# The mean made once, inner values on 128 partitions, and a diagonal in two parts, in the LayerNorm of a four-layer kernel

## The chip, the cores and the metric

The kernel runs on one core of a Trainium2 chip. The metric is device time in microseconds of that core, median of the timed runs. A core has TensorE (PE, with its weight load PEld), VectorE (DVE), ScalarE (ACT), GpSimd (POOL) and SyncE (SP), each with its own instruction queue worked off in order.

## The reference

Input x is 8 sequences of 256 tokens of 256 values. Four layers each add to it: L0 (two routed ReLU experts and three shared ones, mixed by a gate), L1 (eight SiLU-gated experts and a shared one), L2 and L3. The change lies in L2, and in one place where L0 ends:

```python
h = relu(x @ w1[lang] + b1[lang])          # 256 -> 64
y = x + h @ w2[lang] + b2[lang]            # 64 -> 256
mean = jnp.mean(y, axis=-1, keepdims=True)
var = jnp.mean(jnp.square(y - mean), axis=-1, keepdims=True)
x = x + (y - mean) * rsqrt(var + 1e-5) * gamma[lang] + beta[lang]
x = x + x @ W3[subject].T + b3[subject]    # L3
```

## The kernel before

Activations are held transposed, features on 128 partitions in two tiles (`dt` 0 and 1), tokens along the free dimension. Most products are made in fp32r from a high and a low part of each operand: `xh` and `xl` are rounded x and the rest, and `product` (L435 to L437) issues high by high, high by low, low by high. ScalarE makes high parts, VectorE or GpSimd the low parts (`lo_part`, L1440).

The last phase runs L1's shared expert over five jobs (`LAST_JOBS`): three of 512 tokens and two of 256, eight steps each, T = 0 to 39. In step T TensorE issues `last_up(T)` (12 products), then `last_down(T-2)` (6 products), then the hooks of T. VectorE in step T makes the gated tile and its low part (`last_tile`), and in the first step of a job, inside `last_tile`, `last_take` of the job before, which waits for all of its down products and adds them to x. Then come its hooks. Steps 40 and later hold only the rest. As `last_down` lags two steps, TensorE issues the last down products of a job in the second step of the next one.

L2 and L3 are hung in as hooks per unit (unit 0 to 4 = job 0 to 4). The table `WHEN` gives for each unit the step T of each stage, in the order of `STAGES`, and every engine takes its own stages of step T, ordered by unit, then by stage: x2 (high ScalarE, low VectorE), xs (row sum of x in two parts, units 1 and 2: GpSimd, ScalarE, GpSimd), up (TensorE, 64 rows out), hid (ScalarE ReLU twice: plain into `ru`, rounded into `u`; VectorE the low part), down (TensorE), res (VectorE adds x and bias), square (VectorE, GpSimd), scale (ScalarE), var (TensorE), eps (VectorE, then GpSimd takes the power -0.5), diag (ScalarE: identity times the inverse deviation, 128x128 for every 128 tokens), rstd (TensorE spreads it over the partitions), norm and add (VectorE), x3 (high) and x3l (low), l3a and l3b (TensorE), outa and outb (VectorE). Units 0 to 2 use the PSUM pair `sums[0]`, unit 3 `up_ps[:, 2:4]`.

The weights W2 are centred, so that only the mean of x has to be taken off. In the down stage (`l2_down_stage`) `mean_part` adds -1/256 times the column sums of x to both output tiles, and the three products with the 64-row weights follow. b2 is centred in `center_b2` (VectorE, step 10). Unit 4, `END`, is spread over the steps from 42 on in a form of its own.

L0's mix of the last 512 tokens is made by VectorE inside L1's first pairs, k = 0 to 3 (`pair_tiles`): `gate_probs` and `mix`.

## Time and profile before

| | |
|---|---|
| median of 3 runs | 1599.67 us (1598.49 to 1599.91) |
| the profiled execution, device time | 1598.26 us |
| its span, first to last instruction | 1596.5 us |
| TensorE busy | 1583.3 us, 99% |
| VectorE / ScalarE / GpSimd busy | 71% / 58% / 41% |
| mean granted TensorE clock, DMA | 1.000, mean 54 GB/s |

Busy times add up overlapping matmuls, so 99% does not say that TensorE is at its peak. The chain of waits says what the end hangs on, and the list of waits says where an engine stood still and which instruction ended it. In a timeline a line gives start, duration, engine, source line and, in brackets, the idle time ahead of it and who ended it.

### The profile page before, as it was taken

The numbers are of one execution on the slowest core, as the hardware profiler recorded it, in microseconds if no ns is written. First come the engines' busy times: TensorE is split into PE (matmuls) and PEld (weight loads), VectorE is DVE, ScalarE is ACT, GpSimd is POOL, SyncE is SP. The second block draws the span as 40 slices with busy tenths as digits, with TensorE's granted clock in tenths as the row PEclk, the third lists the DMA queues.
The fourth block names the chain that finished last, engine by engine and source line by source line (L and its number), as shares of the span: only waits on it lengthen the run. The fifth ranks groups of instructions, "written<-read, shape, count | busy, mean of one in ns | idle before, by whom it ended". The sixth has DMA issues, their size and how long they took to land.

```text
span 1596.5 us, 22398 instructions
## 1 busy us (share of the span) xinstructions
PE 1583.3 (99%) x7944; PEld 1345.9 (84%) x7944; DVE 1138.5 (71%) x1676; ACT 930.0 (58%) x1680; POOL 662.1 (41%) x576
## 2 busy tenths in 40 slices
PE   9999999999999999999999999999999999999999
PEld 7888888999987888888888888888888888888888
DVE  6755557778889777777776777777777777656556
ACT  5655555665665665565565565565565565554343
POOL 7765544655775431431431431431431431146110
PEclk9999999999999999999999999999999999999999
DMA  4111105455421010010010010010010010021000
GB/s 159 54 54 53 54 27 181 164 185 173 159 84 36 14 41 27 14 40 27 14 40 28 14 40 27 14 40 28 14 41 27 14 40 27 28 58 51 14 14 27
DMA packets 30500, 85.46 MB, mean 54 GB/s; under 512 B 5030, under 2 KB 10022, under 8 KB 30262
## 3 DMA queue, kind: packets, MB, share of 16 engines
q1 hardware_dynamic: 29798, 82.68, 15.1%
q8 instruction: 63, 1.03, 0.3%
q0 software_dynamic: 304, 1.10, 0.2%
q14 instruction: 47, 0.39, 0.1%
q10 hardware_dynamic: 288, 0.26, 0.1%
HBM read 81.93 MB, written 2.10 MB: 53 GB/s over the span
## 4 chain that ended last, share of the span: by engine, by line
PE 93%; DVE 4%; POOL 2%; issue 1%; ACT 1%; DMA 0%; SPq 0%; ACTq 0%; DVEq 0%; POOLq 0%
PE up L666 13%; PE up L668 13%; PE up L667 13%; PE sum L435 12%; PE sum L436 12%; PE sum L437 12%; PE up L435 3%; PE up L436 3%; PE up L437 3%; PE up L443 2%; PE up L444 2%; PE up L445 2%; DVE expert_out L2004 1%; POOL shared_up L1440 1%; DVE hidden L2018 1%
## 5 line engine op out<-in xcount | busy, mean ns | idle before, releaser
L1265 ACT ACTIVATE hidden_hi<-up_tile 128x512 fp32r<-128x512 f32 x256 | 161.2, 630 | 187.7 <-DVE up_tile L2062 163.7
L2057 DVE TENSOR_TENSOR gate_tile<-up,gate_tile 128x512 f32<-128x512 f32 x192 | 129.9, 687 | 141.7 <-PE up L668 141.7
L2067 DVE TENSOR_TENSOR hidden_lo<-up_tile,hidden_hi 128x512 fp32r<-128x512 f32 x256 | 196.7, 788 | 44.7 <-ACT hidden_hi L1265 44.7
L666 PE MATMUL up<-x_sums,gate_up 128*128 128x512 f32 x512 | 199.3, 389 | 0.0
L435 PE MATMUL sum<-hidden_hi,down 128*128 128x512 f32 x512 | 199.3, 389 | 0.0
L437 PE MATMUL sum<-hidden_hi,down 128*128 128x512 f32 x512 | 199.3, 389 | 0.0
L436 PE MATMUL sum<-hidden_lo,down 128*128 128x512 f32 x512 | 199.2, 389 | 0.0
L668 PE MATMUL up<-x_sums,gate_up 128*128 128x512 f32 x512 | 199.2, 389 | 0.0
L667 PE MATMUL up<-x_sums,gate_up 128*128 128x512 f32 x512 | 199.2, 389 | 0.0
L2062 DVE TENSOR_TENSOR up_tile<-up_tile,gate_tile 128x512 f32<-128x512 f32 x192 | 183.8, 983 | 2.3
L1258 ACT ACTIVATE gate_tile<-gate_tile 128x512 f32<-128x512 f32 x192 | 119.7, 632 | 90.4 <-DVE gate_tile L2057 88.3
L1440 POOL TENSOR_TENSOR gate_up<-raw,gate_up 128x384 fp32r<-128x384 f32 x60 | 68.0, 1133 | 204.2 <-ACT gate_up L1209 204.2
L1254 ACT ACTIVATE gate_tile<-up 128x512 f32<-128x512 f32 x192 | 110.6, 594 | 71.2 <-PE up L668 64.8
L666 PE MATMUL up<-x_hi,gate_up 128*128 128x512 f32 x384 | 149.7, 390 | 0.9 <-DVE up_tile L2062 0.9
L667 PE MATMUL up<-x_lo,gate_up 128*128 128x512 f32 x384 | 149.4, 389 | 0.0
L668 PE MATMUL up<-x_hi,gate_up 128*128 128x512 f32 x384 | 149.4, 389 | 0.0
L2057 DVE TENSOR_TENSOR up_tile<-up,up_tile 128x512 f32<-128x512 f32 x192 | 130.0, 687 | 2.6 <-PE up L668 0.7
L1440 POOL TENSOR_TENSOR expert_in<-raw,expert_in 128x512 fp32r<-128x512 f32 x64 | 92.1, 1440 | 89.4 <-ACT expert_in L975 89.3
L1254 ACT ACTIVATE up_tile<-up 128x512 f32<-128x512 f32 x192 | 112.1, 600 | 21.2 <-PE up L668 15.6
L1567 POOL TENSOR_TENSOR weight_sums<-raw 128x256 f32<-128x256 f32 x30 | 28.9, 964 | 204.7 <-PE up L668 204.7
L435 PEld LDWEIGHTS sum<-hidden_hi,down 128*128 128x128 f32 x512 | 96.1, 188 | 20.8 <-DVE hidden_lo L2067 1.2
L666 PEld LDWEIGHTS up<-x_sums,gate_up 128*128 128x128 f32 x512 | 96.1, 188 | 20.3 <-ACT gate_tile L1254 0.4
(323 smaller groups left out, 4031.2 us busy)
## 6 DMA issues: line engine op xcount, KB each, us to landing
raw<-in_experts SPq DMA_DIRECT2D x64, 512.0 KB, 3.2
raw<-in_l SPq DMA_DIRECT2D x51, 512.0 KB, 3.2
raw<-in_shared SPq DMA_DIRECT2D x23, 512.0 KB, 3.3
raw<-in_w SPq DMA_DIRECT2D x8, 256.0 KB, 2.6
x<-in_xT SPq DMA_DIRECT2D x3, 512.0 KB, 9.1
l_stage<-in_l SPq DMA_DIRECT2D x3, 512.0 KB, 4.1
out<-out_stage SPq DMA_DIRECT2D x6, 256.0 KB, 2.6
gate_w<-in_gw POOLq DMA_DIRECT2D x1, 1024.0 KB, 6.1
```

The lines of the kernel that those rows point to most:

```text
L435: pe.matmul(out, wh, vh, start=start, stop=False)
L436: pe.matmul(out, wh, vl, start=False, stop=False)
L437: return pe.matmul(out, wl, vh, start=False, stop=stop)
L666: pe.matmul(out, wh, vh, start=first, stop=False, skip_group_check=True)
L667: pe.matmul(out, wh, vl, start=False, stop=False, skip_group_check=True)
L668: return pe.matmul(out, wl, vh, start=False, stop=True, skip_group_check=True)
L1254: A(out, ps, ACT.Copy).then_inc(q_done[m], 1)
L1265: A(hi[:, i], cu[:, i], ACT.Copy).then_inc(hi_done, 1)
L1440: return nc.gpsimd.tensor_tensor(dst, src, hi.bitcast(f32), ALU.subtract)
L2057: V.tensor_tensor(t, ps, t, ALU.add).then_inc(c_done[m], 1)
L2062: V.tensor_tensor(cu[:, i], up, cg[:, RING[i]], ALU.mult).then_inc(gat_done, 1)
L2067: V.tensor_tensor(lo[:, i], cu[:, i], hi[:, i].bitcast(f32), ALU.subtract).then_inc(lo_done, 1)
```

## The change

- Units 0 to 3: the product of x with -1/256 is made once, into output tile 1, in a new stage `mean` (TensorE). VectorE adds it to both tiles of x, into `y`, ahead of its part of hid; res adds `y` instead of x. The last unit keeps both mean products.
- W2 is loaded twice, on partitions 0 to 63 and 64 to 127, and centred and rounded on all 128. `u` holds high values on partitions 0 to 63 and low values on 64 to 127. One product with 128 rows takes the place of two with 64; the product with W2's low part stays at 64 rows.
- The diagonal is rounded to fp32r by ScalarE, VectorE makes its rest (`diaglo`), and the spread is two fp32r products with rounded ones. It is issued between the up and the down products of its step.
- The table `WHEN` is changed, and the waits at the up and mean stages for the output copies.
- In L1's pair k = 1 the gate's probabilities and the experts' mix come earlier in VectorE's queue; the low part is added by GpSimd, and VectorE waits for that in k = 2.
- Two products of ones are issued in the very first up product.

```diff
-STAGES = ["x2", "xs", "up", "hid", "down", "res", "square", "scale", "var", "eps", "diag", "rstd",
+STAGES = ["x2", "xs", "up", "mean", "hid", "down", "res", "square", "scale", "var", "eps", "diag", "diaglo", "rstd",
           "norm", "add", "x3", "x3l", "l3a", "outa", "l3b", "outb"]
 WHEN = [dict(zip(STAGES, at)) for at in (
-    (9, 10, 11, 11, 12, 12, 12, 13, 13, 13, 13, 14, 14, 14, 15, 15, 16, 16, 17, 18),
-    (17, 18, 19, 19, 20, 20, 20, 21, 21, 21, 21, 22, 22, 22, 23, 23, 24, 25, 25, 26),
-    (25, 26, 27, 28, 29, 29, 29, 30, 31, 31, 32, 33, 33, 35, 35, 36, 37, 37, 38, 38),
-    (34, 34, 35, 35, 36, 36, 36, 37, 37, 37, 38, 39, 43, 43, 45, 45, 46, 48, 46, 50))]
+    (9, 10, 11, 11, 11, 12, 12, 12, 13, 13, 13, 13, 14, 15, 15, 15, 16, 16, 17, 17, 17, 18),
+    (17, 18, 19, 19, 19, 20, 20, 20, 21, 21, 21, 21, 22, 23, 23, 23, 24, 24, 25, 25, 25, 26),
+    (25, 26, 27, 27, 28, 29, 29, 29, 30, 31, 31, 32, 33, 34, 34, 35, 35, 36, 37, 37, 38, 38),
+    (34, 34, 35, 35, 35, 37, 37, 37, 38, 38, 38, 39, 40, 41, 43, 43, 45, 45, 46, 48, 46, 50))]
 for u in (0, 3):
     del WHEN[u]["xs"]
...
-    w2 = [place(f"l2_w2_{b}", [A2, 2, D], f32r, over=where_in, skip=2 * K1 * at)
+    w2 = [place(f"l2_w2_{b}", [2 * A2, 2, D], f32r, over=where_in, skip=2 * K1 * at)
...
-    diag = place("rstd_diag", [P, 4, P], f32, over="shared_sums", skip=4 * B * D)
+    diag = place("rstd_diag", [P, 4, P], f32r, over="shared_sums", skip=4 * B * D)
...
+    diag_lo = place("rstd_diag_lo", [P, 4, P], f32r, over="raw", skip=6144)
+    ones_r = place("ones_r", [P, P], f32r)
...
+    u = place("l2_hidden_r", [2 * A2, BLK], f32r, over="raw", skip=10240)
...
                 sp.dma_start(raw[:, s, 512:640], w1_d[langs[b]]).then_inc(raw_full[s], 16)
-                sp.dma_start(raw[0:A2, s, 640:896], w2_d[langs[b]]).then_inc(raw_full[s], 16)
...
+                    for _ in range(2):
+                        pe.matmul(up_ps[:, 3, 0:P], ones[:], ones[:], start=True, stop=True)
...
                 if i in (1, 2):
-                    pe.wait_ge(out_ready, 2 * i)
-                if i == 4:
-                    pe.wait_ge(out_ready, 6)
+                    pe.wait_ge(out_ready, 2 * i - 1)
+                if i == END:
+                    pe.wait_ge(out_ready, 5)
...
                 out = unit_ps[i][:, m, c0:c0 + n]
-                if "xs" in WHEN[i]:
-                    for part in range(2):
-                        pe.matmul(out, minus_mean[:], xsr[i // 2][:, part, 0:n], start=part == 0, stop=False, skip_group_check=True)
-                    return
                 for dt in range(DT):
                     for part in (xh, xl):
                         pe.matmul(out, minus_mean[:], part[:, dt, t0:t0 + n], start=dt == 0 and part is xh, stop=False,
                                   skip_group_check=True)

-            def l2_down_stage(i):
-
-                b0, nb, t0, c0, n = unit(i)
+            def mean_stage(i):
+
+                b0, nb, t0, c0, n = unit(i)
+                out = unit_ps[i][:, 1, c0:c0 + n]
                 if i == 0:
                     pe.wait_ge(b2_done, 1)
+                if i in (1, 2):
+                    pe.wait_ge(out_ready, 2 * i)
                 if "xs" in WHEN[i]:
                     pe.wait_ge(xs_lo, i)
-                mean_part(i, 1)
+                    pe.matmul(out, minus_mean[:], xsr[i // 2][:, 0, 0:n], start=True, stop=False)
+                    pe.matmul(out, minus_mean[:], xsr[i // 2][:, 1, 0:n], start=False, stop=True).then_inc(mean_done, 1)
+                    return
+                last = product_of_parts(out, t0, n)
+                last.then_inc(mean_done, 1)
+
+            def product_of_parts(out, t0, n):
+
+                for dt in range(DT):
+                    pe.matmul(out, minus_mean[:], xh[:, dt, t0:t0 + n], start=dt == 0, stop=False)
+                    last = pe.matmul(out, minus_mean[:], xl[:, dt, t0:t0 + n], start=False, stop=dt == DT - 1)
+                return last
+
+            def l2_down_stage(i):
+
+                b0, nb, t0, c0, n = unit(i)
                 if i == END:
+                    pe.wait_ge(out_ready, 6)
+                    mean_part(i, 1)
                     x_part(i, 0)
                 pe.wait_ge(hid_relu, i + 1)
-                mean_part(i, 0)
+                if i == END:
+                    mean_part(i, 0)
+                else:
+                    pe.wait_ge(x_centered, i + 1)
                 pe.wait_ge(l2_hid, i + 1)
                 for b in range(b0, b0 + nb):
                     c = slice(b % 2 * S, (b % 2 + 1) * S)
                     for m in range(DT):
                         out, k = unit_ps[i][:, m, c], slice(m * P, (m + 1) * P)
-                        pe.matmul(out, w2[b][:, 0, k], u[:, 0, c], start=False, stop=False, skip_group_check=True)
-                        pe.matmul(out, w2[b][:, 0, k], u[:, 1, c], start=False, stop=False, skip_group_check=True)
-                        last = pe.matmul(out, w2[b][:, 1, k], u[:, 0, c], start=False, stop=True, skip_group_check=True)
+                        pe.matmul(out, w2[b][:, 0, k], u[:, c], start=i != END, stop=False, skip_group_check=True)
+                        last = pe.matmul(out, w2[b][0:A2, 1, k], u[0:A2, c], start=False, stop=True, skip_group_check=True)
                 last.then_inc(l2_down, 1)
                 if i == END:
...
                 b0, nb, t0, c0, n = unit(i)
+                out, q = unit_ps[i][:, 1, c0:c0 + n], slice(c0 // P, (c0 + n) // P)
                 pe.wait_ge(diag_done, i + 1)
-                pe.matmul(unit_ps[i][:, 1, c0:c0 + n], ones[:],
-                          diag[:, c0 // P:(c0 + n) // P].rearrange("p q n -> p (q n)"),
-                          start=True, stop=True).then_inc(rstd_bc, 1)
+                pe.wait_ge(diag_low, i + 1)
+                pe.matmul(out, ones_r[:], diag[:, q].rearrange("p q n -> p (q n)"), start=True, stop=False)
+                pe.matmul(out, ones_r[:], diag_lo[:, q].rearrange("p q n -> p (q n)"),
+                          start=False, stop=True).then_inc(rstd_bc, 1)

...
                         pair_up(e, j, s)
-            hooks = placed({"up": l2_up_stage, "down": l2_down_stage, "var": var_stage,
-                            "rstd": rstd_stage, "l3a": lambda i: l3_stage(i, 0), "l3b": lambda i: l3_stage(i, 1),
+            hooks = placed({"up": l2_up_stage, "mean": mean_stage, "down": l2_down_stage, "var": var_stage,
+                            "l3a": lambda i: l3_stage(i, 0), "l3b": lambda i: l3_stage(i, 1),
                             "beta": beta_part, "scaled": scaled_part})
             hooks.setdefault(10, []).insert(0, b2_stage)
+            within = placed({"rstd": rstd_stage})

             def last_step(T, tok, N):
...
                 last_up(T, tok, N)
+                for h in within.get(T, []):
+                    h()
                 if T == 0:
                     pair_down(NSS - 1, 1)
...
-                    last = A(u[:, 0, c], unit_ps[i][0:A2, 0, c], ACT.Relu, bias=b1[:, b:b + 1])
+                    last = A(u[0:A2, c], unit_ps[i][0:A2, 0, c], ACT.Relu, bias=b1[:, b:b + 1])
                 last.then_inc(hid_relu, 1)
...
                 gate_up_lo(e, 3)
+                if e == 0:
+                    pool.wait_ge(x_experts, 2)
+                    last_block = slice((NB - 1) * BLK, NB * BLK)
+                    G(x[:, :, last_block], x[:, :, last_block], xl[:, :, last_block].bitcast(f32), ALU.add).then_inc(x_low_added, 1)
                 down_lo(e, 2)
...
                 lo_part(w1r[:, b, 1], raw[:, s, 512:640], w1r[:, b, 0])
-                lo_part(w2[b][:, 1], raw[0:A2, s, 640:896], w2[b][:, 0]).then_inc(w_lo, 1)
+                lo_part(w2[b][0:A2, 1], raw[0:A2, s, 640:896], w2[b][0:A2, 0]).then_inc(w_lo, 1)

             def row_sum(i):
...
                                                  ALU.mult, ALU.add)
-                if part != NSH - 1:
+                if part == "experts" and tb == NB:
+                    ins.then_inc(x_experts, 1)
+                elif part != NSH - 1:
                     linked(ins)
                 elif b == 1:
...
                 tile_lo(k, 0)
+                if k == 1:
+                    gate_probs(NB)
+                    mix("experts", 0)
+                    mix("experts", 1)
                 if k == 2:
+                    dve.wait_ge(x_low_added, 1)
                     mix(0, 0)
                     mix(0, 1)
...
                     gate_hidden(NB)
-                if k == 1:
-                    gate_probs(NB)
-                    mix("experts", 0)
-                    mix("experts", 1)
...
                 tile_lo(k, 1)
-                if k == 1:
-                    mix("lo", 0)
-                    mix("lo", 1)
                 if k == 2:
...
-                w = raw[0:A2, s, 640:896]
+                w = raw[:, s, 640:896]
                 linked(V.tensor_reduce(w2s[:], w, AX.X, ALU.add))
-                V.scalar_tensor_tensor(w, w2s[:].to_broadcast([A2, D]), -1.0 / D, w, ALU.mult,
+                V.scalar_tensor_tensor(w, w2s[:].to_broadcast([2 * A2, D]), -1.0 / D, w, ALU.mult,
                                        ALU.add).then_inc(w2_centered, 1)

             def center_b2():

                 V.tensor_scalar(minus_mean[:], ones[:], -1.0 / D, None, ALU.mult)
+                V.tensor_scalar(ones_r[:], ones[:], 1.0, None, ALU.mult)
                 dve.wait_ge(b2_sum, 1)
...
                 c = slice(c0, c0 + n)
+                if i != END:
+                    dve.wait_ge(mean_done, i + 1)
+                    if i:
+                        dve.wait_ge(x3_done, DT * i)
+                    for dt in range(DT):
+                        last = V.tensor_tensor(y[:, dt, c], x[:, dt, t0:t0 + n], unit_ps[i][:, 1, c], ALU.add)
+                    last.then_inc(x_centered, 1)
                 dve.wait_ge(hid_relu, i + 1)
-                V.tensor_tensor(u[:, 1, c], ru[:, c], u[:, 0, c].bitcast(f32), ALU.subtract).then_inc(l2_hid, 1)
+                V.tensor_tensor(u[A2:2 * A2, c], ru[:, c], u[0:A2, c].bitcast(f32), ALU.subtract).then_inc(l2_hid, 1)

             def res_stage(i):

                 b0, nb, t0, c0, n = unit(i)
                 dve.wait_ge(l2_down, i + 1)
-                if i:
-                    dve.wait_ge(x3_done, DT * min(i, 3))
+                if i == END:
+                    dve.wait_ge(x3_done, DT * 3)
+                else:
+                    dve.wait_ge(x_centered, i + 1)
                 for dt in range(DT):
                     for b in range(b0, b0 + nb):
                         c = slice(b % 2 * S, (b % 2 + 1) * S)
+                        xc = x[:, dt, b * S:(b + 1) * S] if i == END else y[:, dt, c]
                         last = V.scalar_tensor_tensor(y[:, dt, c], unit_ps[i][:, dt, c], b2c[:, b, dt:dt + 1],
-                                                      x[:, dt, b * S:(b + 1) * S], ALU.add, ALU.add)
+                                                      xc, ALU.add, ALU.add)
                     last.then_inc(centered, 1)

...
                 V.tensor_scalar(var[:, qs], unit_ps[i][:, 1, qs], 1.0 / D, 1e-5, ALU.mult, ALU.add).then_inc(var_eps, 1)
+
+            def diag_lo_stage(i):
+
+                b0, nb, t0, c0, n = unit(i)
+                dve.wait_ge(diag_done, i + 1)
+                for q in range(c0 // P, (c0 + n) // P):
+                    last = V.scalar_tensor_tensor(diag_lo[:, q], ident[:], rstd[:, q:q + 1], diag[:, q].bitcast(f32),
+                                                  ALU.mult, ALU.subtract)
+                last.then_inc(diag_low, 1)

             def norm_stage(i):

...
                             "hid": hid_stage, "res": res_stage, "square": square_stage, "eps": eps_stage,
+                            "diaglo": diag_lo_stage,
...
-        "w2": v["L2_cond_W2"],
+        "w2": np.concatenate([v["L2_cond_W2"], v["L2_cond_W2"]], axis=1),
```

## Rows read from the trace of the kernel before

**Rows 1.** The page, part 4: the chain that ended last, shares by engine.
```profile
PE 93%; DVE 4%; POOL 2%; issue 1%; ACT 1%; DMA 0%; SPq 0%; ACTq 0%; DVEq 0%; POOLq 0%
```
**Rows 2.** TensorE's waits: who waited for whom, us in total, times, longest.
```profile
PE sum L435 <- issue: 1.5, 1, 1.5
...
PE up L666 <- DVE up_tile L2062: 0.9, 1, 0.9
...
PE up L814 <- ACT l_hidden_r L1384: 0.8, 1, 0.8
```
**Rows 3.** The chain in order of time: start, us, what; mean and spread products.
```profile
1468.86 1.21 PE sum L814 x4
...
1481.10 0.86 PE sum L856 x2
...
1547.87 0.92 PE sum L810 x4
```
**Rows 4.** Timeline of TensorE (start, us, engine, line), unit 3's down stage.
```profile
1570.19 0.28 PE L814 MATMUL up<-x_hi,minus_mean 128*128 128x256 f32 x1
1570.31 0.28 PE L814 MATMUL up<-x_lo,minus_mean 128*128 128x256 f32 x1
...
1571.64 0.28 PE L436 MATMUL up<-x_lo,last_gate_up 128*128 128x256 f32 x1
```
**Rows 5.** Timeline of the weight loads, first 64-row load of unit 0.
```profile
1469.99 0.18 PEld L834 LDWEIGHTS sum<-l_hidden_r,l_w 64*128 64x128 f32 x1 [0.37 <-issue]
```
**Rows 6.** Timelines of VectorE and GpSimd in L1's pairs k = 1 and 2.
```profile
476.67 1.37 DVE L2057 TENSOR_TENSOR gate_tile<-up,gate_tile 128x512 f32<-128x512 f32 x2 [2.84 <-PE up L668]
482.65 1.54 DVE L1986 SCALAR_TENSOR_TENSOR x<-x,gate,x_hi 128x512 f32<-128x512 f32 x2
...
493.83 2.55 POOL L1440 TENSOR_TENSOR down<-raw,down 128x512 fp32r<-128x512 f32 x2 [11.23 <-ACT down L1218]
```
**Rows 7.** Timeline of VectorE, units 1 and 2: output copy, low halves.
```profile
1541.21 0.68 DVE L2285 TENSOR_TENSOR out_stage<-sum,l_bias 128x512 f32<-128x512 f32 x1
...
1547.79 0.68 DVE L2191 TENSOR_TENSOR l_hidden_r<-l_hidden,l_hidden_r 64x512 fp32r<-64x512 f32 x1 [1.02 <-ACT l_hidden_r L1384]
...
1571.41 1.29 DVE L2183 TENSOR_TENSOR x_lo<-x,x_hi 128x512 fp32r<-128x512 f32 x2
```
**Rows 8.** Timeline of VectorE, steps 15 and 16: x3l of unit 0, last_take.
```profile
1487.42 1.29 DVE L2183 TENSOR_TENSOR x_lo<-x,x_hi 128x512 fp32r<-128x512 f32 x2
...
1495.71 1.66 DVE L2140 SCALAR_TENSOR_TENSOR x<-sum,l_coef,x 128x256 f32<-128x256 f32 x4 [4.12 <-PE sum L437]
```
**Rows 9.** Timelines: unit 0's last up product, and the end of center_b2.
```profile
1463.52 0.28 PE L437 MATMUL sum<-x_hi,l_w 128*64 128x256 f32 x1
...
1464.68 0.17 DVE L2175 SCALAR_TENSOR_TENSOR b_centered<-b_sum,l_cols 128x16 f32<-128x16 f32 x1
```
**Rows 10.** Timelines: 128-column subtraction, unit 2's spread, low part of tile 33.
```profile
1536.33 0.48 DVE L2245 TENSOR_TENSOR x_lo<-l_cols,x_hi 128x128 fp32r<-128x128 f32 x2
...
1560.34 1.12 PE L856 MATMUL sum<-rstd_diag,ones 128*128 128x512 f32 x2 [0.23 <-ACT rstd_diag L1400]
...
1561.83 0.43 DVE L2156 TENSOR_TENSOR hidden_lo<-up_tile,hidden_hi 128x256 fp32r<-128x256 f32 x1 [0.49 <-ACT hidden_hi L1342]
```
**Rows 11.** Timelines: unit 3's diagonal, last up product, start of last_down(39).
```profile
1578.83 0.68 ACT L1400 ACTIVATE rstd_diag<-ident,rstd 128x128 f32<-128x128 f32 x2
...
1580.91 0.28 PE L437 MATMUL up<-x_hi,last_gate_up 128*128 128x256 f32 x1
...
1583.04 0.39 PE L435 MATMUL sum<-hidden_hi,last_down 128*128 128x256 f32 x1
```
**Rows 12.** Timeline of TensorE in the first 11 us.
```profile
6.55 0.80 PE L456 MATMUL up<-x_hi,shared_up 128*128 128x512 f32 x1 [0.78 <-ACT x_hi L1034]
...
10.13 0.63 PE L435 MATMUL up<-x_hi,shared_up 128*128 128x512 f32 x1
...
10.87 0.39 PE L437 MATMUL up<-x_hi,shared_up 128*128 128x512 f32 x1
```

19 lines of the change are left out of this document (12 added, 7 removed).

## The prediction

> **What bounds the kernel now.** I read the chain of waits first: TensorE carries 93% of it [rows 1], so the time is the length of TensorE's own instruction stream plus the places where that stream stands still. Next the list of what TensorE waited for; three of its ten entries, the ones shown, and the wait for the diagonal [rows 10] stand at code that the change edits [rows 2]. Last the timelines of single engines around the LayerNorm stages, because what decides is the order in each engine's queue. Back to back, a product of 512 columns starts 0.23 us after the one before it [rows 3] and one of 256 columns 0.12 us after [rows 4]. The duration in a row (0.28 us there) is longer because neighbours overlap, so I use distances between starts.
>
> **Sum, part 1: TensorE's own products.** Four products of -1/D with 512 columns take 0.92 us [rows 3]. Making the mean once saves four of them in unit 0, two each in units 1 and 2 (there it is made from the row sum) and four of 256 columns in unit 3; the last unit keeps both. That is 8x0.23 + 4x0.12 = 2.3 us. The broadcast of the inverse deviation in plain fp32 costs 0.86 us at 512 columns [rows 3], half of it at 256. Two fp32r products cost 2x0.23 and 2x0.12, so it saves 3x0.40 + 0.19 = 1.4 us.
>
> The down products are not the saving they look like. There are fewer, two for three, but the first now has 128 contraction rows and the second still 64, and they alternate. What a change of height costs can be read where unit 3 goes from the 128-row mean products to the six 64-row products and back [rows 4]: from the start of the last mean product (1570.31) to the start of the second product after the return (1571.64) is 1.33 us. That span holds eight distances, so 8x0.12 = 0.95 by the pace, and 0.39 are left for two changes of height: 0.2 each. The weight load of such a product shows how: it starts at 1469.99, the same instant as its product, after 0.37 us of idling, and not one product ahead as the others do [rows 5]. The same excess stands in all five units. The Trainium skill, TensorEngine Tiling (Array Packing), section Tiling Modes, says that changing the tiling mode drains TensorE; by this rule every alternation pays (the sum below), without it none would (rival A), and the trace agrees for the two changes per unit that it has. Before, a 512-column unit costs 12x0.12 + 2x0.2 = 1.84 us. After, eight products and eight changes (seven inside, one on leaving) cost 8x0.12 + 8x0.2 = 2.56. A 256-column unit goes from 1.12 to 4x0.12 + 4x0.2 = 1.28. Sum: 3x0.72 + 2x0.16 = +2.5 us. Part 1 is -2.3 - 1.4 + 2.5 = -1.2 us.
>
> **Part 2: waits of before that go.** (a) In pair k=1 of layer 1 TensorE stood 0.86 us because VectorE's gate probabilities and expert mix (1.54 us) came ahead of the fourth gated tile [rows 2, 6]. They move to a place where VectorE waits for TensorE for 2.84 us, about what they need. With the restart of the pipeline, 0.1 to 0.2 us after each such stop, -1.1. The low part goes to GpSimd, 2.55 us by two 128x512 subtractions, ahead of these, for which it sat idle over 11 us [rows 6]. VectorE asks for it in pair k=2, some 6 us later. Cost nothing; if that cover were gone, up to 2.6. (b) Unit 2's up products waited 1.5 us [rows 2] for the second output copy of unit 1 [rows 7]. They now wait for the first copy, 3 us earlier; only the mean needs the second one and the row sum's low part, both done when it is reached: -1.7 with the restart. (c) The mean products that stood behind ScalarE's ReLU: 0.8 us in unit 3 [rows 2] and 1.21 for 0.92 in unit 0 [rows 3], -1.2 with the restart. (d) Unit 2's broadcast waited 0.2 for the diagonal [rows 10]: -0.4. Together -4.4.
>
> **Part 3: waits that come.** (a) Job boundaries. In units 0 and 1 the low half of x3 (x3l) moves from steps 15 and 23 to 16 and 24, and l3a to 17 and 25. Steps 16 and 24 are the first tiles of a new job, and there VectorE's own code first does last_take, which waits for last_down(15) and last_down(23). TensorE issues these in steps 17 and 25, immediately ahead of l3a. So l3a now waits for: semaphore 0.2, last_take 1.66, first half of the split 0.6; a second half later its other products go on. In the trace last_take stands behind 4.12 us of idling, and the split had been made at 1487 [rows 8]. From the end of the down products: 0.2 + 1.6 + 2x0.6 = 3.0, less 0.36 of products done between the halves: 2.7 us, twice: +5.4. Behind that wait in VectorE's queue stand only tiles with slack. (b) mean_stage(0) comes right behind the up products of step 11, which end at 1463.63, but must wait for b2_done, whose last instruction ends at 1464.85, plus 0.1 for the new copy of ones [rows 9]; with semaphore and restart +1.55. (c) Unit 2's first down product now reads hi and lo together, so the mean no longer covers the low half. That half came at 1548.5, when TensorE was in the 0.92 us of mean products that began at 1547.87 [rows 3, 7]. Counted from step 28, TensorE now stands there 0.92 us sooner, and VectorE's two additions of 0.6 us, 1.0 of which fit into its idle time ahead of the low half, make that 0.2 later: +1.1. In units 0 and 1 a step of 4.08 us lies between, in unit 3 l3a(2): nothing. (d) Unit 2's diaglo runs on VectorE behind tile 33, which ended at 1562.26 [rows 10]. Its four products of identity and deviation, 128 columns each, have no row of their own: the nearest are 0.24 us by a 128-column subtraction [rows 10] and 0.41 by the 256-column products of last_take [rows 8]. I take 0.28, near the first, which has their size. So it ends near 1563.4. TensorE, which had come to the broadcast 0.4 us before it could start at 1560.34 [rows 10], comes one step's up products later (12x0.12 = 1.44), at 1561.4: +2.1 (bounds 1.9 to 2.6). In units 0 and 1 a step is 4.08 us instead of 2.16 and it just fits: +0.1 each (0 to 0.6). (e) l3a(2) was covered by unit 3's down stage, which moves from step 36 to 37 behind it. VectorE's split, which ended at 1572.6 [rows 7], keeps its place in VectorE's chain while TensorE comes 2.6 us earlier: +1.4. (f) Unit 3's broadcast now stands ahead of last_down(39). That product started 2.0 us after the end of the up products, right behind the low tile of step 39 [rows 11]. Now ScalarE's diagonal (0.68 [rows 11]) in place of VectorE's low tile beside it (0.43), diaglo's two products (0.56), the two semaphores and the broadcast itself (0.24) come in between: +1.2, and all that follows to the end starts later by it. Sum: 5.4 + 1.55 + 1.1 + 2.1 + 0.2 + 1.4 + 1.2 = +13.0 us (bounds 10 to 15).
>
> **Part 4: edits with a small or no cost.** The start: two fp32 products of ones fill the 0.78 us before L456 [rows 12]. TensorE's clock is at the lower of its levels (1.2 GHz) there and rises at 10.8 us: a product takes 0.63 us at 10.13 and 0.39 at 10.87 [rows 12], 4.2 us after the wait's end at 6.55. No row shows what the clock does without that stop. Either it rises as before (0), or as much sooner as the stop and the product ahead of it lasted, 1.6 us, and four products take half (-0.8). I take -0.4, the middle. The centring of W2 and its high part on 128 partitions instead of 64 work on as many columns, and the DMA issues are as many: 0. VectorE's two additions per unit (1.2 us) lie in gaps of 1 to 4 us in units 0 and 1 and are priced in (c) and (e) for the others.
>
> **Total.** -1.2 - 4.4 + 13.0 - 0.4 = +7.0 us. The profiled execution took 1598.26 us with a span of 1596.5, so it would take 1605.3; the median of the three runs lies 1.4 above it, and 1599.67 + 7.0 = 1606.7.
>
> **Rivals.** (A) A change of height costs only once per unit, or only with other instructions around it. For it: the trace shows no alternation. Against: ten changes of ten pay, in both directions. By the Trainium skill's rule above, each one would. Down costs 8x0.12 = 0.96 (512) and 0.48 (256) at its best: 3x0.9 + 2x0.64 = 4.0 us gained instead of 2.5 lost: +0.5, 1600.2 us. (B) The other side, faster: the queues of VectorE keep ahead. If the split of x3 is there when last_down(15) ends, and the diagonals too, none of part 3 comes and only TensorE's stream counts: -1.2 - 4.4 - 0.4 = -6.0, 1593.7 us. It decides at steps 17 and 25: up to 7 us less of new waits the kernel is no longer slower. For it: VectorE has idle time in every step. Against: what is late is an order in a queue, not load. (C) The new waits are dearer: additions that read PSUM and run beside GpSimd's work stretch, or TensorE's clock falls after a 2.5 us stop, which the 1.5 us stop of before did not do. 15 us of waits instead of 13 and some 2 us at half clock: 1611. (D) The change does not do what it says: the broadcast in two parts, or the copy on the upper 64 partitions, makes instructions of another cost: within 2 us of the forecast on either side.
>
> **How the numbers follow.** Forecast with its own spread of 1603 to 1609.5: 0.68. (D) 0.04. (A) 0.12. (B) 0.08. (C) 0.08. The range of 8 in 10 takes in the forecast and most of (A) and leaves out (B) and the upper part of (C): 1600.5 to 1610. About 0.2%, 3.2 us, is what a measurement of this kernel can tell from no change. Slower by more than that (above 1602.9): 0.68 + 0.03 (D) + 0.08 (C) = 0.79. Within it: (A) and the low edge of the others, 0.12. Faster: (B) and a little of (A), 0.09.
>
> **What would show it.** L856's two fp32 records per unit become two lines of 0.23 us. In the down stage, starts 0.3 us apart with weight loads that start with their product (right), or 0.12 apart (A). Waits of TensorE: two of 2.5 us at l3a of units 0 and 1, released by VectorE's split behind last_take; 1.4 at unit 0's mean; 2 us at unit 2's broadcast, released by diaglo; 1 us at down(2) and 1.4 at l3a(2); none at up(2), none at L666 in k=1. If l3a of units 0 and 1 starts without a wait, my reading of the queue order is wrong, and with it the sign. At the start, spacing of 0.23 us before 10.8 us shows the earlier clock.

## The result, and the profile after

The changed kernel takes 1618.36 us (median of four runs, 1614.25 to 1619.84) against 1599.08 of the kernel before (four runs, 1596.78 to 1599.91): ratio 1.0118, 95% interval 1.0102 to 1.0134, 19.3 us slower. I had forecast 1606.7, that is +7.0, with a range to 1610. The sign was right and the size was not. The profiled execution took 1618.27 us with a span of 1616.5, 20.0 more than that of before. All ratios compare executions in the fast state; of those below only one of e13, at 5198.85 us, was not.

TensorE's waits of the changed kernel, the lines that answer to [rows 2] (who waited for whom: us in total, times, longest):

```profile
PE sum L899 <- DVE x_lo L2220: 7.9, 5, 2.4
...
PE sum L839 <- DVE b_centered L2212: 2.4, 1, 2.4
PE sum L883 <- DVE rstd_diag_lo L2272: 1.9, 1, 1.9
PE up L883 <- DVE rstd_diag_lo L2272: 1.3, 1, 1.3
...
PE sum L860 <- DVE l_hidden_r L2235: 1.0, 1, 1.0
...
PE up L440 <- DVE x_lo L2220: 0.5, 1, 0.5
PE up L673 <- POOL gate_up L1472: 0.4, 1, 0.4
PE sum L440 <- DVE hidden_lo L2105: 0.3, 1, 0.3
```

Every stop that I forecast is there, at its place and with its releaser; the wait of 1.5 us at up(2) is gone. So the queue reading held, except in L1's pair k=1, where I had forecast no wait and two short ones are left (0.4 and 0.3, the last two lines). What I did not have is in another column: TensorE's granted clock, in stretches of 2 us (PE busy, clock, DMA share, GB/s):

```profile
1466.00:1468.00 2.00, 1.83 (x4) 0.56 0.00 0
1468.00:1470.00 2.00, 2.00 (x7) 0.59 0.00 0
...
1500.00:1502.00 2.00, 1.03 (x4) 0.59 0.00 0
1502.00:1504.00 2.00, 2.00 (x10) 0.50 0.00 0
1504.00:1506.00 2.00, 2.00 (x12) 0.50 0.14 49
1506.00:1508.00 2.00, 2.00 (x9) 0.70 0.28 91
...
1548.00:1550.00 2.00, 2.00 (x12) 0.54 0.02 4
1550.00:1552.00 2.00, 2.00 (x13) 0.61 0.39 131
...
1564.00:1566.00 2.00, 2.00 (x8) 0.81 0.01 4
1566.00:1568.00 2.00, 2.00 (x11) 0.50 0.00 0
1568.00:1570.00 2.00, 2.00 (x17) 0.84 0.00 0
```

Everywhere else from 1440 us to the last product, and in the same stretches of the kernel before, it is 1.00. Four times the clock falls to its lower level (1.2 of 2.4 GHz), each time behind a new stop. I call this half clock, and give it as the time lost by it: one minus the clock, times 2 us. Summed over these eleven lines it is 8.5 us. On the page the row PEclk still shows a 9 in every slice, since a slice is 40 us long. Only narrow windows show the fall. It is not the same in every execution: the mean granted clock was 0.994 in three of the four and 0.997 in the one that took 1614.25 us. The windows, and what I say below of half clock, are of the one profiled execution of each kernel.

To see where the 20 us arise I read the start of the first up product of each step in the timelines of both kernels. The first up product of unit 0 starts at the same instant in both:

```profile
1462.26 0.28 PE L440 MATMUL sum<-x_hi,l_w 128*64 128x256 f32 x1
```

(in the kernel before it is L435 at 1462.26). So nothing of the 20 us, in either direction, lies ahead of it, and "tail" below is the time from there to the last product of the kernel: 131.18 us before, 151.17 after. It leaves out the way to that point, which ends between 1462.3 and 1464.3 us in the profiles below, whatever was changed. A tail is always that of the one profiled execution of a kernel.

### The profile page after: what moved, and what is told of

It is laid out like the page before. It is cut to its first block, busy times and chain, and to the rows that moved or that the text cites. A ratio compares the mean times of both kernels' runs of the same rounds, so it can differ in the third digit from the quotient of the medians.

```text
span 1616.5 us, 22393 instructions
## 1 busy us (share of the span) xinstructions
PE 1590.8 (98%) x7920; PEld 1350.6 (84%) x7920; DVE 1152.3 (71%) x1697; ACT 930.4 (58%) x1680; POOL 665.7 (41%) x577
## 4 chain that ended last, share of the span: by engine, by line
PE 90%; DVE 5%; POOL 2%; issue 1%; ACT 1%; DMA 0%; SPq 0%; ACTq 0%; POOLq 0%; DVEq 0%
PE up L673 12%; PE up L674 12%; PE up L675 12%; PE sum L440 12%; PE sum L441 12%; PE sum L442 12%; PE up L440 3%; PE up L441 3%; PE up L442 3%; PE up L448 2%; PE up L449 2%; PE up L450 2%; DVE expert_out L2042 1%; POOL shared_up L1472 1%; DVE hidden L2056 1%
```

## The experiments

**e4: the stop alone.** Kernel before, one move:

```diff
-    (9, 10, 11, 11, 12, 12, 12, 13, 13, 13, 13, 14, 14, 14, 15, 15, 16, 16, 17, 18),
-    (17, 18, 19, 19, 20, 20, 20, 21, 21, 21, 21, 22, 22, 22, 23, 23, 24, 25, 25, 26),
+    (9, 10, 11, 11, 12, 12, 12, 13, 13, 13, 13, 14, 14, 14, 16, 16, 17, 17, 17, 18),
+    (17, 18, 19, 19, 20, 20, 20, 21, 21, 21, 21, 22, 22, 22, 24, 24, 25, 25, 25, 26),
```

> The kernel before with one thing changed: x3's two parts and l3a of units 0 and 1 one step later (x3l in steps 16 and 24, l3a in 17 and 25), as in the changed kernel. Theory: two stops of 2.35 + about 1 us at l3a, and half clock behind each, 3.4 and 1.7 us: 10 to 12 us slower than before, 1609 to 1611. As I forecast (stops alone): 5.4 to 6.7 slower, 1604.5 to 1606. Rival that the stops come from the whole of the change: within 1 us of before.

Measured: 1608.77 us, ratio 1.0057 (1.0040 to 1.0073), +9.3 us; tail +8.80. The stops are those of the changed kernel (timeline of TensorE):

```profile
1498.34 0.39 PE L872 MATMUL sum<-l_w,x_hi 128*128 128x256 f32 x1 [2.35 <-DVE x_lo L2183]
1500.02 0.58 PE L872 MATMUL sum<-l_w,x_hi 128*128 128x256 f32 x1 [1.06 <-DVE x_lo L2183]
...
1543.97 0.39 PE L872 MATMUL sum<-l_w,x_hi 128*128 128x256 f32 x1 [2.35 <-DVE x_lo L2183]
1545.65 0.38 PE L872 MATMUL sum<-l_w,x_hi 128*128 128x256 f32 x1 [1.06 <-DVE x_lo L2183]
```

3.4 us of half clock stand behind the first pair and none behind the second, though the two pairs are alike. By step starts the first boundary costs 6.6 us and the second 2.2: of its 3.9 (below) 1.7 are taken back, because up(2) of before had to wait anyway. x3, its low part and l3a one step later in two units, without any other part of the change, make nearly half of its loss.

**e3: the stop taken out of the changed kernel.** Units 0 and 1 go back to their former steps, and their broadcast stands behind last_down again:

```diff
-    (9, 10, 11, 11, 11, 12, 12, 12, 13, 13, 13, 13, 14, 15, 15, 15, 16, 16, 17, 17, 17, 18),
-    (17, 18, 19, 19, 19, 20, 20, 20, 21, 21, 21, 21, 22, 23, 23, 23, 24, 24, 25, 25, 25, 26),
+    (9, 10, 11, 11, 11, 12, 12, 12, 13, 13, 13, 13, 13, 14, 14, 14, 15, 15, 16, 16, 17, 18),
+    (17, 18, 19, 19, 19, 20, 20, 20, 21, 21, 21, 21, 21, 22, 22, 22, 23, 23, 24, 25, 25, 26),
```

> The changed kernel with units 0 and 1 put back to the steps of the kernel before from the low diagonal to the output (rstd 14 and 22, x3l 15 and 23, l3a 16 and 24), low diagonal in steps 13 and 21; all other edits stay. Theory: the stops behind last_take (2.35 + 0.94 and 2.35 + 1.06 us) go and with them the half clock behind them (5.1 us): 11 us faster than the changed kernel, about 1607, less what the low diagonal costs in its earlier place (0 to 1.5). Rival without the clock: 6.7 us faster, about 1611.7. Rival that the stops come back in another place of VectorE's queue: under 4 us.

Measured: 1609.69 us, ratio 1.0065 (1.0048 to 1.0082), 8.7 less than the changed kernel; tail 9.8 less. The stops at l3a of units 0 and 1 are gone. Not all came back as time: the low diagonal in its earlier place costs waits of 0.19 and 0.23 us, unit 2's mean now waits 1.0 us for the low part of the row sum, which the stop had covered, and 3.4 us of half clock are left, behind mean(0) and unit 2's down stage.

**e2: the stops stay, TensorE is kept busy.** In the changed kernel:

```diff
+                    pe.wait_ge(gated_done, 11)
+                    for _ in range(9):
+                        pe.matmul(up_ps[:, 0], w3[0][:, 0, 0:P], w3[0][:, 0, 0:BLK], start=True, stop=True)
                     pe.wait_ge(b2_done, 1)
...
+                if i < 2 and part == 0:
+                    for _ in range(9):
+                        pe.matmul(unit_ps[i][:, 0], w3[b0][:, 0, 0:P], w3[b0][:, 0, 0:BLK], start=True, stop=True)
```

> The changed kernel with nine products of 512 columns (9x0.23 = 2.1 us, results thrown away) put ahead of mean(0) and of l3a in units 0 and 1, where TensorE otherwise stands 2.4 us; what releases it comes no sooner. Theory: half clock for some 17 us behind the stops costs 8.5 us of the changed kernel, 6.8 of them behind these three stops; with TensorE kept busy the clock stays at 1.00 there and the kernel is some 6.8 us faster (1611 to 1612). If the clock falls because of something else than the stop, such as the current of the stage that follows, it is the same to within 1 us or slower by the fillers.

Measured: 1614.09 us, ratio 1.0092 (1.0075 to 1.0109), 4.3 less, not 6.8. Half clock is gone at the three places, though what releases TensorE comes no sooner (mean(0) at 1466.79). But 3.4 us of it now stand in another place, behind unit 2's down stage, where the changed kernel lost 1.7 (this is the profiled execution, 1614.77 us with a mean clock of 0.997; two of the three others took 1613.3 and 1613.4 us with 0.999, so they can have had little half clock):

```profile
1558.00:1560.00 2.00, 2.00 (x6) 0.81 0.00 0
1560.00:1562.00 2.00, 2.00 (x7) 0.50 0.02 4
1562.00:1564.00 2.00, 2.00 (x11) 0.50 0.00 0
1564.00:1566.00 2.00, 2.00 (x12) 0.50 0.00 0
```

**e15: seven stops filled.** As e2, with three such products also in the second stop of l3a (units 0 and 1), four ahead of down(2) and eight ahead of unit 2's broadcast, 45 products in all (the text below says six stops; both stops of l3a in two units, mean(0), down(2) and the broadcast are seven):

```diff
+            def keep_busy(count, done=24):
+
+                pe.wait_ge(gated_done, done)
+                for _ in range(count):
+                    pe.matmul(up_ps[:, 2], w3[0][:, 0, 0:P], w3[0][:, 0, 0:BLK], start=True, stop=True)
```

> The changed kernel with products of 512 columns (results thrown away) in six of its stops: mean(0), both stops of l3a in units 0 and 1, down(2) and the broadcast of unit 2; every release stays where it is, so only the clock can gain. Theory: no half clock behind step 10, 8.5 us less than the changed kernel (1618.4), 1610. If the fillers of e2 only moved the half clock to a later stop, and it moves on to the last two (l3a(2), broadcast of unit 3): 1611.6 or 1613.3, as e2.

Measured: 1613.19 us (1611.98 to 1614.85), ratio 1.0091 (1.0077 to 1.0104). The profiled execution took 1611.98, 6.3 less than that of the changed kernel, and shows 1.00 in every window of the tail: 144.27 us, 6.9 less. Unit 0's l3a in the timeline (nine and three filling products, x9 and x3), and the windows where the changed kernel had 0.50:

```profile
1496.42 2.20 PE L906 MATMUL sum<-l_w 128*128 128x512 f32 x9
1498.94 0.38 PE L917 MATMUL sum<-l_w,x_hi 128*128 128x256 f32 x1 [0.31 <-DVE x_lo L2238]
1499.39 0.85 PE L815 MATMUL up<-l_w 128*128 128x512 f32 x3
```

```profile
1502.00:1504.00 2.00, 2.00 (x16) 1.00 0.00 0
1504.00:1506.00 2.00, 2.00 (x11) 1.00 0.38 131
```

The stage with alternating heights is still there, so the half clock is tied to the stops. It is worth 6.9 us and not 8.5; I take it that a part falls on time in which TensorE waits for VectorE all the same. And a tail of 13.1 us over before remains at full clock. The clock is a third of the 20.0 us, and about half of the 13.0 by which I missed them.

**e10: half the stop.** The kernel of e4 with five filling products ahead of each l3a (the second diff of e2 with `range(5)`).

> The kernel of e4 (before, with x3l and l3a of units 0 and 1 one step later) with five products of 512 columns ahead of l3a, so that the first stop of each unit is about 1.2 us instead of 2.35, the second (1.05) as it is; the release is no sooner. Theory, clock lost only behind a stop that is long by itself: no half clock, 3.4 us less than e4 (1608.8), 1605.4. Rival, any two stops of some 1 us in a row suffice: as e4, 1607 to 1609.

Measured: 1607.65 us, ratio 1.0053 (1.0039 to 1.0067); tail +7.62, 1.2 less than e4. Stops of 1.22 and 1.05 in unit 0 brought no half clock, the same pair (1.22 and 1.06) in unit 1 brought 1.7 us:

```profile
1542.35 0.41 PE L875 MATMUL sum<-l_w,x_hi 128*128 128x256 f32 x1 [1.06 <-DVE x_lo L2186]
```

```profile
1542.00:1544.00 2.00, 1.65 (x8) 0.64 0.00 0
1544.00:1546.00 2.00, 2.00 (x12) 0.50 0.02 4
```

Neither theory holds as written. Two stops of about 1 us in a row can be enough, and need not be. The first boundary, without half clock, costs 3.9 us by step starts, as in e15, though half of its first stop is filled: the release comes no sooner.

**e6 and e7: the down stage alone.** In the kernel before, the two-product form only. e6 alternates 128 and 64 rows as the change does; e7 has the low weights on 128 partitions too (their upper copy meets the low hidden values, which adds a term that was left out), so that nothing alternates:

```diff
-                        pe.matmul(out, w2[b][:, 0, k], u[:, 0, c], start=False, stop=False, skip_group_check=True)
-                        pe.matmul(out, w2[b][:, 0, k], u[:, 1, c], start=False, stop=False, skip_group_check=True)
-                        last = pe.matmul(out, w2[b][:, 1, k], u[:, 0, c], start=False, stop=True, skip_group_check=True)
+                        pe.matmul(out, w2[b][:, 0, k], u[:, c], start=False, stop=False, skip_group_check=True)
+                        last = pe.matmul(out, w2[b][0:A2, 1, k], u[0:A2, c], start=False, stop=True, skip_group_check=True)
```

and from e6 to e7:

```diff
-                        last = pe.matmul(out, w2[b][0:A2, 1, k], u[0:A2, c], start=False, stop=True, skip_group_check=True)
+                        last = pe.matmul(out, w2[b][:, 1, k], u[:, c], start=False, stop=True, skip_group_check=True)
-                lo_part(w2[b][0:A2, 1], raw[0:A2, s, 640:896], w2[b][0:A2, 0]).then_inc(w_lo, 1)
+                lo_part(w2[b][:, 1], raw[:, s, 640:896], w2[b][:, 0]).then_inc(w_lo, 1)
```

> The kernel before with the two-product down stage alone: first product 128 rows, second 64 rows, as in the changed kernel; the mean stays made twice, nothing is moved. Theory (a change of height costs 0.2 us each time): 0.72 us more in each of three units and 0.16 in two, +2.5 us, 1602; with half clock behind unit 2's down stage another 1.7 or 3.4. Rival (A of the prediction, height changes free): two products for three and 3.9 us less, 1595.6.

> The same, with the second product over 128 rows as well, so that nothing alternates and no change of height is left: 3x(1.84-0.96) + 2x(1.12-0.48) = 3.9 us less than before, 1595.6. If the height has nothing to do with it, the same time as the kernel of the run before, whatever that is.

Measured: e6 1600.97 us, ratio 1.0015 (1.0005 to 1.0024), tail +2.38; e7 1596.32 us, ratio 0.9980 (0.9971 to 0.9990), tail -2.72. The same number of products, and 5.1 us between their tails (4.7 between the medians). e6 confirms the term of +2.5. e7 misses by 1.2: unit 0's down stage is 0.75 shorter, and right behind it TensorE waits 0.5 us for GpSimd's square sums, so that 0.59 comes back one step later. Neither kernel shows any half clock: alternation alone does not lower it.

**e1: the same repair in the changed kernel** (the diff from e6 to e7).

> The changed kernel with its second down product (low weights) also read over 128 rows, so that no product of the down stages has another height than its neighbours; the number of products stays the same. If each change of height costs 0.2 us, three units go from 8x0.3 us to 8x0.12 and two from 4x0.3 to 4x0.12: 6.4 us less, and up to 1.7 us more if the stretch at half clock behind unit 2's down stage goes with it: 6.4 to 8.1 us faster than the changed kernel (1618.4), so 1610 to 1612. Rival: the spacing of 0.3 us comes from the number of rows or from the waits around it, not from the alternation: within 1 us of the changed kernel.

Measured: 1610.12 us, ratio 1.0066 (1.0049 to 1.0083), 8.2 less; tail 8.4 less, with 5.1 us of half clock instead of 8.5. Those 3.4 us are not shown to be the work of the edit: mean(0), which stands ahead of every edited product, had its stop of 2.38 us as before and lost nothing behind it here, and 1.7 in the changed kernel. Unit 2's down stage in the changed kernel, and then in e1 (starts of neighbours):

```profile
1563.11 0.38 PE L861 MATMUL sum<-l_hidden_r,l_w 64*128 64x256 f32 x1
1563.42 0.39 PE L860 MATMUL sum<-l_hidden_r,l_w 128*128 128x256 f32 x1
1563.74 0.38 PE L861 MATMUL sum<-l_hidden_r,l_w 64*128 64x256 f32 x1
```

```profile
1559.55 0.28 PE L861 MATMUL sum<-l_hidden_r,l_w 128*128 128x256 f32 x1
1559.66 0.28 PE L860 MATMUL sum<-l_hidden_r,l_w 128*128 128x256 f32 x1
1559.78 0.28 PE L861 MATMUL sum<-l_hidden_r,l_w 128*128 128x256 f32 x1
```

0.31 us apart where the height changes, 0.12 where it does not: 0.19 for each change.

**e5: b2 one step earlier.** The changed kernel with `hooks.setdefault(9, []).insert(0, center_b2)` for 10 on VectorE.

> The changed kernel with center_b2 one step earlier in VectorE's queue (step 9, where VectorE idles 0.86 us for x_hi, instead of 10). Theory: b2_done is there when TensorE comes to mean(0), the stop of 2.38 us goes, and with it the 1.7 us lost at half clock right behind it: 2.4 to 4.1 us faster than the changed kernel (1618.4). If the half clock only moves to a later stop: 2.4. Rival that TensorE waits for something else there (the row of -1/D, the PSUM half): no gain.

Measured: 1616.13 us, ratio 1.0103 (1.0086 to 1.0120), 2.2 less; tail 2.95 less. The stop of 2.38 is gone, down(0) now waits 1.10 for the low hidden half, which had been covered by it, and half clock fell from 8.5 only to 6.8 us. The stop itself had been dearer than my 1.55 for a reason that the changed kernel's VectorE shows:

```profile
1464.49 0.22 DVE L2209 TENSOR_SCALAR ones_r<-ones 128x128 fp32r<-128x128 f32 x1
1464.63 0.17 DVE L2211 TENSOR_REDUCE b_sum<-sum 128x8 f32<-128x16 f32 x1
1464.83 1.28 DVE L2212 SCALAR_TENSOR_TENSOR b_centered<-b_sum,l_cols 128x16 f32<-128x16 f32 x1
```

and GpSimd's timeline beside it:

```profile
1464.82 2.36 POOL L1472 TENSOR_TENSOR l_w<-raw,l_w 128x512 fp32r<-128x512 f32 x3 [2.65 <-ACT l_w L1385]
```

The copy of ones delayed an operation of 16 columns by 0.15 us, so that it began 0.01 us behind GpSimd's subtraction instead of 0.13 ahead of it, and it took 1.28 us instead of 0.17 [rows 9]. The traces of all 17 kernels agree: where it began 0.01 or 0.02 us behind a subtraction of GpSimd it took 1.28 to 1.32 us (ten kernels, e5 among them), where it began with it (e11) or up to 0.13 ahead, 0.17 or 0.18 (seven). The Trainium skill, Perfetto Trace Analysis, section Optimizing Scalar/DVE Operations, says that GpSimd and VectorE share an SBUF read port, and these rows agree with it; I did not run the operation without GpSimd beside it.

**e9: the edits that only take a stop away.** Kernel before with the two products at the start, the expert mix of k=1 moved, and `pe.wait_ge(out_ready, 2 * i - (i == 2))` at up(2).

> The kernel before with the three edits that only fill or take away a stop: two products of ones at the start, expert mix of k=1 before the fourth tile with its low part on GpSimd, up(2) behind the first output copy of unit 1 (the mean behind the second). Theory: start -0.8 us (half clock ends some 4 us sooner), k=1 from 0.86 to 0.4 + 0.3, so -0.2, up(2) -1.5 to -1.7: 2.5 to 2.7 us less than before, about 1596.9. Rival that TensorE only comes sooner to a later wait (the row sum's low part, ReLU of unit 2): 1 to 1.5 us less.

Measured: 1597.55 us, ratio 0.9989 (0.9980 to 0.9998), -1.8; tail -1.73, all of it in one step, at up(2). The other two bring nothing. From the wait for expert_out (the first one behind 370 us) to up(0) the kernel before takes 1085.30, the changed kernel 1085.23 us, with 0.86 us of stop at k=1 in the one and 0.41 + 0.27 in the other. At the start the changed kernel is 0.8 ahead, and at 377 us no longer:

```profile
45.77 0.47 PE L448 MATMUL up<-x_hi,shared_up 128*128 128x512 f32 x1 [0.48 <-POOL shared_up L1472]
...
377.03 0.36 PE L440 MATMUL sum<-hidden,expert_out 128*128 128x256 f32 x1 [0.31 <-DVE expert_out L2042]
```

In the kernel before the same two rows start at 46.59 and 376.96. And the 0.8 is no effect of the edit: in e6 and e7, which lack it, the first row starts at 45.58 and 45.59, in e9, which has it, at 46.77.

**e11: the two-part broadcast alone.** Kernel before, low diagonal in steps 13, 21, 32 and 38:

```diff
-                pe.matmul(unit_ps[i][:, 1, c0:c0 + n], ones[:],
-                          diag[:, c0 // P:(c0 + n) // P].rearrange("p q n -> p (q n)"),
-                          start=True, stop=True).then_inc(rstd_bc, 1)
+                pe.wait_ge(diag_low, i + 1)
+                pe.matmul(out, ones_r[:], diag[:, q].rearrange("p q n -> p (q n)"), start=True, stop=False)
+                pe.matmul(out, ones_r[:], diag_lo[:, q].rearrange("p q n -> p (q n)"),
+                          start=False, stop=True).then_inc(rstd_bc, 1)
```

> The kernel before with the broadcast of the inverse deviation in two fp32r parts alone, in all four units, low part right behind the high one (steps 13, 21, 32, 38). TensorE's stream gets 1.4 us shorter. Theory: the low part costs 4x0.28 us on VectorE, hidden in units 0 and 1, but in unit 2 behind last_take and in unit 3 in TensorE's way: waits of about 1.2 and 1.0 us more, so +0.8 us, 1599.5 to 1601. Rival that the low part is hidden everywhere: 1.4 us less, 1598.

Measured: 1601.38 us, ratio 1.0015 (1.0006 to 1.0024), +2.0; tail +1.81. Of it 1.5 us are in unit 2, where the low part waits behind last_take; in units 0 and 1 waits of 0.18 and 0.21 us eat up what the shorter products save:

```profile
1564.37 0.47 PE L861 MATMUL sum<-rstd_diag,ones_r 128*128 128x512 f32 x1 [2.11 <-DVE rstd_diag_lo L2231]
```

Unit 3, for which I had put 1.0, shows no loss. The part is a loss on its own in these places, for the most part at one step.

**e13: three repairs together.** The diffs of e1, e3 and e5 in one kernel.

> The changed kernel with three repairs at once: second down product over 128 rows (e1), units 0 and 1 in their former steps (e3), b2 centred one step earlier (e5); mean once, two-part diagonal and the moved steps of units 2 and 3 stay. Alone they gave 8.2, 8.7 and 2.3 us. If the time of half clock is tied to these stops, all of it goes: 1618.4 less 8.5 of half clock, 4.8 of alternation, 6.1 of stops at l3a, 2.4 less 1.1 of stop at mean(0) and down(0): 1597.7. If some half clock only moves behind the stops of units 2 and 3 that remain (1.0, 1.9, 1.2, 1.3 us), 1599.4 or 1601.

Measured: 1600.11 us, ratio 1.0003 (0.9994 to 1.0012); tail +0.73, with 1.7 us of half clock, now behind unit 2's broadcast, whose stop of 1.92 had brought none in the changed kernel:

```profile
1562.91 0.47 PE L883 MATMUL sum<-rstd_diag,ones_r 128*128 128x512 f32 x1 [1.92 <-DVE rstd_diag_lo L2275]
```

```profile
1562.00:1564.00 2.00, 1.09 (x6) 0.93 0.00 0
1564.00:1566.00 2.00, 2.00 (x12) 0.50 0.00 0
```

The three places repaired here carry the 19 us. What is left of the change is a draw.

**e8, e12 and e14: the gains without the stops.** e8 is the changed kernel with 128 rows in both down products, b2 early, the kernel before's steps in units 0 and 1, and in units 2 and 3 the former mean made twice and the fp32 diagonal (a flag `ONCE = 2`). e12 makes VectorE's low hidden half ahead of the additions, and of the down products only those into output tile 1, which overwrite the mean, wait for the additions:

```diff
-                        pe.matmul(out, w2[b][:, 0, k], u[:, c], start=i != END, stop=False, skip_group_check=True)
+                        pe.matmul(out, w2[b][:, 0, k], u[:, c], start=i < ONCE, stop=False, skip_group_check=True)
...
+                    if m == 1 and i < ONCE:
+                        pe.wait_ge(x_centered, i + 1)
```

Its first pair of lines is e8's, the second e12's. e14 makes the mean twice in unit 0 too.

> What gave time without a new wait, put together: two products at start, mix move in k=1, up(2) waiting for the first output copy only, down stage in two products of 128 rows in all units (-3.9), mean once and diagonal in two parts in units 0 and 1 only, in the steps of the kernel before, b2 centred one step earlier; units 2 and 3 keep the mean made twice and the fp32 diagonal. Sum: 0.8 + 0.2 + 1.7 + 3.9 + 1.4 + 0.8 = 8.8 us less than before, 1590 to 1592; every stop that remains above 1 us makes it that much longer and may bring 1.7 or 3.4 us at half clock. Rival that units 0 and 1 must pay for mean and diagonal with stops in any order: 1595 or more.

> The kernel of e8 with one stop less: in unit 0 and 1 VectorE makes the low half of the hidden values ahead of the two additions of the mean, and the down products of the first half of the columns no longer wait for the additions. The wait of 1.11 us at down(0) shrinks to 0.2 to 0.5: 0.6 to 0.9 us less than e8 (1593.4), 1592.5 to 1592.8. Rival that the gain is lost to the wait for the squares behind it (0.67): no difference.

> The kernel of e8 with the mean made twice again in unit 0 (once only in unit 1): no additions ahead of the hidden low half there. Takes away the stop of 1.11 us at down(0) and some 0.3 at the squares, brings back four products (0.92) and the ReLU wait (0.3): within 0.5 us of e8 (1593.4). If the mean made once is worth its price in unit 0: 0.5 slower than e8; if the stop costs more than it shows: up to 1 faster.

Measured: e8 1593.39 us, ratio 0.9960 (0.9946 to 0.9974), tail -4.90; e12 1595.37 us, 0.9976 (0.9967 to 0.9985), tail -3.94; e14 1595.01 us, 0.9975 (0.9965 to 0.9985), tail -5.00. No half clock in any of them. All three are faster than both kernels. e8 fell short of its sum of 8.8: 1.0 of it were the start and k=1, which are worth nothing (e9), 1.2 is what e7 lost behind the square sums, and down(0) waits 1.11 us for the additions. e12 made that worse: 0.94 and 0.52 us of waiting in place of 1.11, and 1.07 at the square sums in place of 0.67. e8 and e14 have the same tail, so making the mean once is worth nothing in unit 0; that e14's median is 1.6 higher lies ahead of the tail (up(0) at 1462.30 in e8 and 1463.99 in e14).

## Where the 20 us are, and which steps of the prediction failed

Starts of the first up product of a step, as difference to the kernel before in us, each with its own difference at step 11 taken off (from the timelines of TensorE):

| step | what lies ahead of it | after | e15, no half clock | e13 | e7 | e8 |
|---|---|---|---|---|---|---|
| 13 | mean(0), down(0) | +3.7 | +2.1 | -0.6 | -0.7 | -0.6 |
| 16 | squares, broadcast of unit 0 | +3.5 | +1.9 | -0.3 | -0.2 | -0.3 |
| 18 | l3a(0) | +9.4 | +5.8 | -0.3 | -0.2 | -0.3 |
| 24 | unit 1 to broadcast | +9.8 | +5.9 | -1.5 | -0.9 | -1.4 |
| 28 | l3a(1), up(2), mean(2) | +14.0 | +8.6 | -1.4 | -0.8 | -3.0 |
| 30 | down(2) | +15.0 | +9.6 | -1.9 | -1.6 | -3.8 |
| 35 | broadcast of unit 2 | +17.7 | +10.9 | -0.3 | -1.5 | -3.7 |
| 39 | l3a(2), down(3) | +18.7 | +11.8 | +0.2 | -2.1 | -4.3 |
| end | broadcast of unit 3, last unit | +20.0 | +13.1 | +0.7 | -2.7 | -4.9 |

**Part 1, products: right where it was measured.** Down stage +2.5 forecast, +2.4 measured alone (e6), 0.19 for each change of height against my 0.2. The sentence of the Trainium skill (TensorEngine Tiling (Array Packing), section Tiling Modes) that a change of mode drains TensorE holds for every one of the alternations, and rival (A) is out. The mean (-2.3) and the broadcast (-1.4) were not measured by themselves over all units. Down products with 128 rows throughout were in none of my terms.

**Part 2, waits that go.** (b) up(2), -1.7 forecast, -1.7 in e9: right. (a) k=1, -1.1 forecast, -0.1 measured: wrong. The step that failed is "They move to a place where VectorE waits": the stop of 0.86 became two of 0.41 and 0.27, at GpSimd's and VectorE's next results. I had named the queue that was relieved and not asked who was next. (c) and (d) have no run of their own; the rows show no wait at ReLU any more.

**Part 3, waits that come: right in place, too small in size.** (a) 2.7 for each boundary where a job begins, measured 3.9 at full clock (e15: +1.9 to +5.8): the failed term is the split, "0.6" for each half. Its row in the changed kernel says 2.36 us for two, 1.18 each, where it now runs beside GpSimd's row sum; against 1.29 for two in its former place [rows 8]. 2x1.2 = 2.4 us. (b) 1.55, measured 2.38, the stretched operation of e5: +0.9 with the restart. (c) 1.1 and 1.0; (d) 2.1 and 1.9; (e) 1.4 and 1.2; (f) 1.2 and 1.3: right. Not in the list: 0.5 us at unit 3's up products for x_lo.

**Part 4, start: -0.4, measured 0.** The clock rose sooner (products of 0.39 us from 7.4 us on, where before they took 0.63 until 10.1) and nothing of it was left at 377 us. The level is read from these durations: the row of the granted clock says 1.00 there in both kernels.

**The clock: the term that failed most.** The main sum has nothing for half clock, since the single stop of 1.5 us of before [rows 2] had brought none. Rival (C) named the fall, with "some 2 us at half clock" in its 1611, and VectorE's additions stretching beside GpSimd's work (it was the split and the b2 operation that did), and got a chance of 0.08. Measured: 6.9 us for the clock alone. (C) had the mechanism and a third of its size, and its 1611 is still 7 us short.

The sum: 7.0 forecast, +6.9 half clock (e15), +1.5 for k=1 and the start, +2.4 split, +0.9 b2, +0.5 up(3), and 0.8 left over that I did not take apart: 20.0. What stays open is why a stop brings half clock in one run and not in another. Over the profiled executions a pair of 2.35 and about 1 us lost 0, 1.7 or 3.4 us, one of 2.38 lost 0 (e1) or 1.7, one of 1.92 lost 0 or 1.7, and nothing in the rows ahead of them tells these apart.

## What to carry to other kernels

Before a stage is moved to another step, look for work that its engine does only in some steps: the first step of a job looks like any other in the table of steps, but VectorE's queue has last_take there, and a split and its user moved onto it cost 9 us. Price a new stop of TensorE at its length plus a share for half clock (here 6.9 us on some 15 us of new stops), ask for every gain upstream what next paces that engine before adding it, and fill both operands to the full height rather than alternate heights.

## What the runs showed of the hardware that I had not expected

The granted clock fell behind stops far shorter than the work around them: once behind 1.22 and 1.06 us with products in between (e10), and behind unit 2's single one of 0.97 us, with products of alternating height following, in all four kernels that have it so (changed kernel, e2, e3, e5), and not when the heights did not alternate (e1, e13); these are too few to show that the heights decide. Each fall lost 1.7 or 3.4 us. Filling the stop with products whose results are thrown away kept the clock at 1.00 (e15), and the kernel got 6.3 us faster by computing 45 products more (profiled executions; 5.2 us by the medians).

A VectorE operation of 16 columns took 0.17 us where it began 0.13 us ahead of a GpSimd subtraction and 1.28 where it began 0.01 behind it, and so in all 17 traces.
